# Ten sample tiles instead of nine in a DLRM interaction kernel, with layer 2 of the first two tiles placed between layers 0 and 1

## The reference, cut to what matters

```
e  = stack([tbl_m[ids[:, m]] for m in range(32)], axis=1)      # b m d
xk = e
for W in (W0, W1, W2):                                          # m h k, k = 64
    xk = relu(einsum('bmd,bhd,mhk->bkd', e, xk, W))
    outs.append(sum(xk, axis=2))
z = concatenate(outs, axis=1)                                   # 512 x 192
h = relu(concatenate([z, dense_ctx], 1) @ W_top1 + b_top1)      # 512
h = relu(h @ W_top2 + b_top2)                                   # 256
y = h @ W_top3
```

## Time and profile before

| | us |
|---|---|
| median of 3 runs | 350.59 (350.45 to 353.13) |
| the profiled execution | 353.74 |
| its span (first to last instruction) | 351.9 |
| TensorE busy | 305.4 (87%) |
| VectorE busy | 274.2 (78%) |
| GpSimd busy | 254.2 (72%) |
| ScalarE busy | 61.6 (18%) |

### The profile page before, as it was taken

How to read it: one execution, slowest core, us unless ns; L and a number is a source line. 1 busy time by engine, 2 the same in 40 slices (tenths; PEclk the granted TensorE clock), 3 DMA queues, 4 the chain that set the end, 5 groups by cost and what they waited for, 6 DMA issues and landing times. The chain is left out here.

```text
span 351.9 us, 3914 instructions
## 1 busy us (share of the span) xinstructions
PE 305.4 (87%) x1476; PEld 112.7 (32%) x1476; DVE 274.2 (78%) x173; ACT 61.6 (18%) x122; POOL 254.2 (72%) x193
## 2 busy tenths in 40 slices
PE   0016859798999988999999999999999999998986
PEld 0013513243334222323333333233333334333426
DVE  0024949799999969999999999999999788954201
ACT  1001210301220330012201220222031104113011
POOL 5775678879788988888898879898919567917000
PEclk9999996999999999999999999999999999999998
DMA  5374956957973984286338643952580102100000
GB/s 178 45 251 83 369 111 180 376 88 213 381 149 65 279 329 80 28 337 260 56 71 303 272 72 77 378 190 61 151 327 0 45 2 63 45 2 0 0 0 0
DMA packets 52282, 52.07 MB, mean 148 GB/s; under 512 B 37574, under 2 KB 42568, under 8 KB 49064
## 3 DMA queue, kind: packets, MB, share of 16 engines
q1 hardware_dynamic: 41272, 39.92, 34.2%
q10 hardware_dynamic: 6896, 10.85, 11.5%
q0 software_dynamic: 4096, 1.06, 3.0%
HBM read 41.33 MB, written 2.10 MB: 123 GB/s over the span
## 5 line engine op out<-in xcount | busy, mean ns | idle before, releaser
L519 DVE TENSOR_TENSOR z_vector<-left,r_forms 128x2048 f32<-128x2048 f32 (+3 forms) x140 | 260.0, 1924 | 45.4 <-DMA r_forms<-x_rows 23.0
L569 PE MATMUL result<-z_vector,w_sb 128*64 128x512 f32 (+2 forms) x1056 | 213.9, 557 | 41.5 <-DVE z_vector L519 40.2
L309 POOL DMA_INDIRECT gathered_rows<-table,row_index x128 | 121.8, 951 | 41.2 <-issue 34.5
L324 POOL TENSOR_TENSOR z_pool<-r_forms,xj_forms 128x1024 f32<-128x1024 f32 (+2 forms) x60 | 131.8, 2232 | 24.7 <-PE result L569 15.0
L569 PEld LDWEIGHTS result<-z_vector,w_sb 128*64 128x64 f32 x1056 | 77.3, 142 | 172.9 <-issue 143.4
L569 PE MATMUL result<-z_pool,w_sb 128*64 128x512 f32 (+2 forms) x240 | 51.8, 571 | 0.0
L384 ACT ACTIVATE x_sb<-result 128x512 f32<-128x512 f32 (+2 forms) x27 | 14.9, 551 | 169.7 <-PE result L569 169.7
L499 DVE TENSOR_REDUCE d_sums<-x_sb 128x32 f32<-128x512 f32 (+2 forms) x27 | 16.8, 625 | 20.0 <-ACT x_sb L384 20.0
L569 PEld LDWEIGHTS result<-z_pool,w_sb 128*64 128x64 f32 x240 | 15.7, 136 | 34.1 <-issue 33.2
L368 ACT ACTIVATE left<-xj_forms 128x512 f32<-128x512 f32 (+2 forms) x36 | 18.6, 547 | 17.1 <-DMA xj_forms<-x_sb 6.8
L359 ACT ACTIVATE left<-h_form 128x512 f32<-128x512 f32 (+2 forms) x18 | 10.0, 553 | 59.8 <-DVE z_vector L519 44.9
(11 more groups left out here) (32 smaller groups left out, 28.1 us busy)
## 6 DMA issues: line engine op xcount, KB each, us to landing
r_forms<-x_rows SPq DMA_DIRECT2D x24, 1024.0 KB, 10.4
r_forms<-x_rows SPq DMA_DIRECT2D x8, 768.0 KB, 6.8
xj_forms<-x_sb ACTq DMA_DIRECT2D x24, 256.0 KB, 4.0
h_form<-x_rows SPq DMA_DIRECT2D x12, 256.0 KB, 3.0
gathered_rows<-table,row_index POOLq DMA_INDIRECT x128, 3.3
r_forms<-x_rows SPq DMA_DIRECT2D x4, 512.0 KB, 6.1
x_rows<-gathered_rows SPq DMA_DIRECT2D x24, 64.0 KB, 2.5
xj_forms<-x_sb ACTq DMA_DIRECT2D x8, 192.0 KB, 3.1
```

The source lines that it names most:

```text
L309: nc.gpsimd.indirect_dma_start(gathered_rows[:, half % GATHERED, g], None, table, bass.IndirectOffsetOnAxis(ap=row_index[:, at:at + 1], ax ...
L324: nc.gpsimd.tensor_tensor(z_pool[:, unit % NZP, t, :, 0:columns(p)], r_form(q, p, t)[:, s0:s1], xj1_forms[form_buffer(n, p)][:, t, 0:colum ...
L519: nc.vector.tensor_tensor(z_vector[:, unit % NV, t, 0:s1 - s0, 0:columns(p)], left[:, t, bank, 0:columns(p)].unsqueeze(1).broadcast_to([12 ...
L569: done = nc.tensor.matmul(result[n][K * t:K * t + K, 0:columns(p)], weights, z[:, t, 0:columns(p)], start=first, stop=last)
```

## The change

The tiles become 8, 16, 24, six of 32, and 16: ten tiles. The order of the first four tiles is written out: (2, 0) comes ahead of (1, 1), and (2, 1) is cut in two, its r0 units ("form 0") between (0, 2) and (1, 2), its r1 units ("form 1") behind (0, 3). From p = 3 on the order is the old one. GpSimd has no products in (1, 0), (2, 0), (1, 1) and (2, 1), and makes the gathers of tiles 0 to 3 (40) ahead of its first product. The other tables of `pool_chunks` move up by one tile with the tiles. ScalarE's and TensorE's orders are written out in the same way.

```diff
-SAMPLES = [16, 24] + [32] * 6 + [24]
+SAMPLES = [8, 16, 24] + [32] * 6 + [16]
...
-STAGES = [(0, 0)]
-for _p in range(NP):
-    STAGES.append((1, _p))
+SPLIT = 1
+STAGES = [(0, 0, "all"), (1, 0, "all"), (0, 1, "all"), (2, 0, "all"), (1, 1, "all"), (0, 2, "all"), (2, 1, "form 0"),
+          (1, 2, "all"), (0, 3, "all"), (2, 1, "form 1")]
+for _p in range(SPLIT + 2, NP):
+    STAGES.append((1, _p, "all"))
     if _p + 1 < NP:
-        STAGES.append((0, _p + 1))
-    if _p > 0:
-        STAGES.append((2, _p - 1))
-STAGES.append((2, NP - 1))
-LAYERS = [_stage for _stage in STAGES if _stage[0] > 0]
-
-GATHERS_FIRST = GATHERS_BEFORE[6]
+        STAGES.append((0, _p + 1, "all"))
+    STAGES.append((2, _p - 1, "all"))
+STAGES.append((2, NP - 1, "all"))
+
+FORM0 = [(_n, _p) for _n, _p, _part in STAGES if _n > 0 and _part != "form 1"]
+FORM1 = [(_n, _p) for _n, _p, _part in STAGES if _part != "form 0"]
+
+GATHERS_FIRST = GATHERS_BEFORE[8]
...
-    few = {(1, 0): 0, (1, 1): 2, (2, 5): 4, (2, 6): 6, (2, 7): 6, (2, 8): 4}
+    few = {(1, 0): 0, (2, 0): 0, (1, 1): 0, (2, 1): 0, (1, 2): 2, (2, 6): 4, (2, 7): 6, (2, 8): 6, (2, 9): 4}
...
@@ GpSimd @@
-            pool.wait_ge(selected, 1)
-            for k in range(4):
-                gather(GATHERS_BEFORE[4] + 4 * k, GATHERS_BEFORE[4] + 4 * k + 4)
-                pool.wait_ge(z_vector_used, k + 2)
+            first = GATHERS_BEFORE[4]
+            pool.wait_ge(selected, selections(1, 0))
+            gather(first, first + 4)
+            pool.wait_ge(z_vector_used, VECTOR_AT[1, 0, 1] + 1)
+            gather(first + 4, first + 8)
+            pool.wait_ge(selected, selections(2, 0))
+            gather(first + 8, first + 12)
+            pool.wait_ge(z_vector_used, VECTOR_AT[0, 1, 0] + 1)
+            gather(first + 12, first + 16)
+            pool.wait_ge(selected, selections(1, 1))
+            gather(first + 16, first + 20)
+            pool.wait_ge(z_vector_used, VECTOR_AT[1, 1, 1] + 1)
+            gather(first + 20, first + 24)
+            pool.wait_ge(selected, selections(2, 1))
+            gather(first + 24, first + 28)
             first = GATHERS_FIRST
-            for n, p in STAGES:
+            for n, p in FORM1:
...
@@ VectorE @@
+            all_products(1, 0, [(0, 0)])
+            products(0, 1, 0)
+            all_products(2, 0, [(1, 0)])
+            all_products(1, 1, [(0, 1), (2, 0)])
+            products(0, 2, 0)
+            products(2, 1, 0)
+            products(2, 1, 1)
+            all_products(1, 2, [(0, 2), (1, 1)])
+            products(0, 3, 0)
+            for k in range(2, len(vector_units(2, 1))):
+                products(2, 1, k)
+            for p in range(SPLIT + 2, NP):
...
@@ TensorE @@
+            layer(1, 0)
+            select(2, 0)
+            vector_unit(0, 1, 0)
+            squares(1)
+            layer(2, 0, {1: [lambda: select(1, 1)]})
+            layer(1, 1)
+            select(2, 1)
+            vector_unit(0, 2, 0)
+            squares(2)
+            vector_unit(2, 1, 0)
+            vector_unit(2, 1, 1)
+            select(1, 2)
+            layer(1, 2)
```

More of the change, by code:

```diff
@@ L86, in pool_units @@
     return units + [(0, s, s + 2) for s in range(4 - max(0, chunks - 4), 4, 2)]
-VECTOR_BEFORE, POOL_BEFORE, STAGE_AT, LAYER_AT = {}, {}, {}, {}
-_v = _w = _l = 0
-for _k, _stage in enumerate(STAGES):
-    VECTOR_BEFORE[_stage], POOL_BEFORE[_stage], STAGE_AT[_stage] = _v, _w, _k
-    if _stage[0]:
-        LAYER_AT[_stage] = _l
-        _l += 1
-    _v += len(vector_units(*_stage))
+VECTOR_AT, POOL_BEFORE = {}, {}
+for _n, _p, _part in STAGES:
+    _count = len(vector_units(_n, _p))
+    for _k in {"all": range(_count), "form 0": range(2), "form 1": range(2, _count)}[_part]:
+        VECTOR_AT[_n, _p, _k] = len(VECTOR_AT)
+_w = 0
+for _stage in FORM1:
+    POOL_BEFORE[_stage] = _w
     _w += len(pool_units(*_stage))
@@ L445, in _ @@
             load_xj1(1, 0)
-            for p in range(NP - 1):
+            copy_xj1(1, 0)
+            copy_h(1)
+            relu(1, 0)
+            load_xj1(2, 0)
+            copy_xj1(2, 0)
+            relu(0, 1)
+            load_xj1(1, 1)
+            copy_xj1(1, 1)
+            relu(2, 0)
+            copy_h(2)
+            relu(1, 1)
+            load_xj1(2, 1)
+            relu(0, 2)
+            load_xj1(1, 2)
+            copy_xj1(1, 2)
+            copy_h(3)
+            relu(1, 2)
+            copy_xj1(2, 1)
+            relu(0, 3)
+            load_xj1(1, 3)
+            load_xj1(2, 2)
+            relu(2, 1)
+            for p in range(SPLIT + 2, NP - 1):
                 copy_xj1(1, p)
@@ L449, in _ @@
                 relu(1, p)
-                if p == 2:
+                if p == SPLIT + 2:
                     load_top()
-                if p > 0:
-                    copy_xj1(2, p - 1)
+                copy_xj1(2, p - 1)
                 relu(0, p + 1)
                 load_xj1(1, p + 1)
-                if p > 0:
-                    relu(2, p - 1)
+                relu(2, p - 1)
                 load_xj1(2, p)
@@ L527, in _, with all_products @@
                                            ALU.mult, ALU.add).then_inc(w0_folded, 1)
-            products(0, 0, 0)
-            for p in range(NP):
-                for k in range(len(vector_units(1, p))):
-                    products(1, p, k)
-                    if k == 1:
-                        sum_d(0, p)
-                        if p == 1:
-                            sum_d(1, 0)
-                        if p == NP - 1:
-                            sum_d(2, p - 2)
+            def all_products(n, p, sums=()):
+                for k in range(len(vector_units(n, p))):
+                    products(n, p, k)
+                    if k == 1:
+                        for of in sums:
+                            sum_d(*of)
+            products(0, 0, 0)
+            all_products(1, 0, [(0, 0)])
[10 more added lines that the diff above has]
+            for p in range(SPLIT + 2, NP):
+                sums = [(0, p)]
+                if p == SPLIT + 2:
+                    sums.append((1, p - 1))
+                if p == NP - 1:
+                    sums.append((2, p - 2))
+                all_products(1, p, sums)
                 if p + 1 < NP:
                     products(0, p + 1, 0)
-                    if p > 1:
-                        sum_d(2, p - 2)
-                if p > 0:
-                    for k in range(len(vector_units(2, p - 1))):
-                        products(2, p - 1, k)
-                        if k == 1:
-                            sum_d(1, p)
+                    sum_d(2, p - 2)
+                all_products(2, p - 1, [(1, p)])
             for k in range(len(vector_units(2, NP - 1))):
@@ L652, in _ @@
             pe.wait_ge(w12_loaded, 16)
-            for p in range(NP - 1):
-                layer(1, p, {1: [lambda: select(2, p - 1)]} if p > 0 else {})
+            layer(1, 0)
[11 more added lines that the diff above has]
+            layer(1, 2)
+            vector_unit(0, 3, 0)
+            squares(3)
+            for k in range(2, len(vector_units(2, 1))):
+                vector_unit(2, 1, k, k == len(vector_units(2, 1)) - 1)
+                if k == 2:
+                    select(1, 3)
+            for p in range(SPLIT + 2, NP - 1):
+                layer(1, p, {1: [lambda: select(2, p - 1)]})
                 vector_unit(0, p + 1, 0)
                 squares(p + 1)
-                if p > 0:
-                    layer(2, p - 1, {1: [lambda: select(1, p + 1)]})
-                else:
-                    select(1, 1)
+                layer(2, p - 1, {1: [lambda: select(1, p + 1)]})
             last = NP - 1
```

23 lines of the change are left out of this document (13 added, 10 removed).

## The result

The changed kernel takes **421.58 us** (median of 4 runs, 420.48 to 421.92), beside 351.01 us for the kernel before on the same chip: ratio 1.196 [1.190, 1.202]. The forecast was 428 us, in a range of 408 to 442. The profiled execution has a span of 420.1 us.

The account below looks back on a forecast made before the run. A loop from GpSimd's late gathers through five engines and queues was taken to bound it: tile 3 at 76.5, plus 46.3, plus four turns of 49.1, plus 2.8 + 114.7 - 7.8, span 428.9, less 1.3: 428 us (408 to 442).

Parts of the forecast that it names:

- E of tile 3: VectorE's end of layer 0 of tile 3, forecast at 76.5 us, bounds 73 and 81.
- to E of tile 4 (no clock loss): First turn of the gather loop, 46.3 us to 122.8; TensorE's idle time before (0, 3) is short, so full clock.
- four turns to E of tile 8: Tiles 5 to 8 each add 49.1 us, together 196.4, so (0, 8) ends at 319.2.
- Where the gathers stand: On GpSimd, tile p's second-half gathers move behind the products of (1, p-1), closing a loop once per tile.
- The length of a turn: Middle: 9.7 + 9.4 + 11.4 + 3.5 + 0.65 + 9.4 + 2.3 = 46.3 us per tile, before clock loss.
- The clock: TensorE's clock halves after each long stall, slowing (0, p): 2.8 us lost per turn, 49.1 us per period.
- The start: First select at about 22.4 us, (1, 2) starts on VectorE at 59.4, (0, 3) ends at 76.5.
- The end: After (0, 8): 2.8 us clock loss plus 114.7 as before, less 7.8 for the smaller last tile.
- A: Rival: the loop binds but TensorE's clock costs little; 414 us, chance 0.18.
- B: Rival: longer loop, all of (0, p) at half clock and landings of 10.8 us; 443 us, chance 0.10.
- C: Rival: gathers early enough, only start and end count, (1, 3) at 83 to 85; 345 to 350 us, chance 0.06.
- D: Rival: start waits shrink, forms keep up, tile 4's second half gathered by about 80 us; 341 us, chance 0.04.

Follow-up runs that it names:

- Late gathers alone: Kernel before, old tiles and layer order, with only GpSimd's gathers hung one product stage later: 422.87 us beside 363.25, ratio 1.164.
- filled run: Changed kernel with unread matmuls added on idle TensorE, 19, 13, 8, 11, 8 pairs for tiles 4 to 8: 415.76 us, ratio 1.173 beside 1.194 unfilled.
- last run with earlier gathers: Rerun of the changed kernel with 16 gathers instead of eight behind the products of (1, 2): 367.88 us beside 361.98, ratio 1.014.
- the sizes alone: Kernel before with only the new tile sizes, old order of stages: 355.55 us beside 352.33, ratio 1.009.
- the run with 17, 12, 8, 9, 8 pairs: Changed kernel with that many pairs of unread matmuls on TensorE ahead of (0, p), tiles 4 to 8: 431.66 us beside 430.54 unfilled.
- first run with earlier gathers: Changed kernel with eight more gathers ahead of GpSimd's first product: 374.7 us beside 363.95 for the kernel before, ratio 1.030.
- the first with 16 gathers behind (1, 2): Changed kernel with 16 gathers instead of eight behind the products of (1, 2), first of two runs: 372.33 us beside 363.25, ratio 1.029.

## Why the prediction was right

The forecast was 427.6, the median is 421.6. By its own steps, E being the end of layer 0 on VectorE:

| step | forecast | measured | off by |
|---|---|---|---|
| E of tile 3 | 76.5 | 79.8 | +3.3 |
| to E of tile 4 (no clock loss) | 46.3 | 45.0 | -1.3 |
| four turns to E of tile 8 | 196.4 | 188.6 | -7.8 |
| from there to the span's end | 109.7 | 106.7 | -3.0 |
| span | 428.9 | 420.1 | -8.8 |

The last line of the sum, the step from span to median, went the other way: I took 1.3 off the span, as before's median stood to its span; here the median is 1.5 above it. So of the 8.8 us by which the span was too long 2.8 were cancelled by luck, and inside the span the late start cancelled 3.3 of 12.1.

**Where the gathers stand: right.** GpSimd idles 12.4 to 14.4 us ahead of the products of (1, 3) to (1, 7), released by xj_forms, VectorE ahead of each (0, p), released by r_forms. Late gathers alone make the loop in the old kernel, earlier gathers take it away in the new one.

**The length of a turn: right in its links, 2 us too long.** In tile 6's turn: from E to the products 9.2 us without the clock's part against 9.7; products 9.37 as taken; gathers to the store 11.2 against 11.4; store to load 3.5 as taken; landing 8.2 against 9.4. The landing is the term that was mis-sized, 1.2 of the 2.1 us: I had read it from r0's loads in the steady middle (9.0, 9.4 and 10.8); in the five stalls it was 7.9 to 8.8. Why r0 lands sooner there no run says.

**The clock: right in kind, somewhat less.** Behind the five stalls the four pairs took 5.65, 6.17, 6.58, 6.58 and 5.21 us where 3.65 is full clock, so 1.6 to 2.9 lost, mean 2.4, where 2.8 was taken. The filled run gives 6.6 us for all five in the time; the intervals of the two ratios leave room for some 2.5 to 12. The Trainium skill ("TensorE: Matmul & The Clock Gate", Part 1) has the ramp under 1% of a typical kernel's span, which would be 4.2 us here. The slow passes add up to 11.9 us or 2.8%, more than that; what they cost in time, 6.6 us or 1.6%, is not clear of 1%, since 4.2 lies between 2.5 and 12.

**The start: 3.3 us too early.** (1, 2) was put at 59.4 on VectorE and began at 62.85, 3.4 us late. Half of it was there when (2, 1)'s first two units ended (57.8, put at 56.1), behind 1.95 us of waiting for tile 2's forms. The other half is the select, for which VectorE stood 5.02 us where 3.3 were allowed. I had given TensorE "about 2 more" at full clock, and its four pairs of (0, 2) were slow:

```profile
53.36 4.49 PE L621 MATMUL result<-z_vector,w_sb 128*64 128x384 f32 x16 [3.58 <-DVE z_vector L559]
```

Four pairs of that size took 2.80 us in the kernel before, at a granted clock of 1.00 (44 to 47 us); here it was 0.50 from 54 to 56 us. These 1.7 us are a fall of the clock in the start, which the sum had left out. (Its 22.4 for the first select should read 22.6, that is 31.61 less 9.0; the gather behind that select came at 22.55.)

**The end: 3.0 us too much.** 1.2 of it is the clock in (0, 8), 1.6 lost instead of 2.8. The other 1.8 lie behind layer 0 of tile 8: from the end of its squares to the end of the span the kernel before needed 110.2 us (from tile 7's squares) and the changed one 100.5, so the smaller last tile was worth 9.7 us where the sum took 7.8. Which stages gave the difference I have not broken down.

**The rivals.** A (the clock costs little, 414) was too low, since passes did slow down, though its number is nearly as close to 421.6 as the forecast. B's landing of 10.8 did not occur. C and D needed the gathers to be free of xj, and those of tiles 4 to 8 were not. C's (1, 3) at 83 to 85 came at 87.25. D's turning point, tile 4's second half gathered by about 80 us, was missed by far: they end at 108.

## What to carry to other kernels

When two producers share one in-order engine, write down for each thing it makes what the instruction ahead of it waits for; if that leads back to the thing's own earlier turn, add up the loop, in transfers and queues as well as in work. A loop of 47 us around engines with 35 us of work decides the time, and every engine in it, even one that is 59% busy, is then on the path. A count that paces one thing by another ("eight gathers behind each stage with products") must be counted anew when stages are moved or stop having products: here 8 gathers one stage earlier were worth 56 to 63 us.

## What the runs showed of the hardware

**Chips differ, most of it in the start.** The kernel before took 351.0 and 352.3 us on two chips and 362 to 364 on two others, one of them used twice (medians). The changed kernel's span on a slower chip was 8.5 us longer than on the first: 6.4 were there at the end of layer 0 of tile 4. On the slower chips the profile shows TensorE, in the first 100 us, standing for nothing it can name ("issue"), and never on the good ones; later labels of this kind there fall on the end of a VectorE product or are under 0.8 us. TensorE's group and first row in the changed kernel on the first chip, and in the last run with earlier gathers, on a slower one:

```profile
L621 PE MATMUL result<-z_vector,w_sb 128*64 128x512 f32 (+3 forms) x1208 | 230.9, 536 | 97.0 <-DVE z_vector L559 95.9
18.62 1.98 PE L621 MATMUL result<-z_vector,w_sb 128*64 128x128 f32 x16 [18.62 <-DVE z_vector L559]
```

```profile
L622 PE MATMUL result<-z_vector,w_sb 128*64 128x512 f32 (+3 forms) x1208 | 225.9, 521 | 44.7 <-issue 27.8
18.96 1.97 PE L622 MATMUL result<-z_vector,w_sb 128*64 128x128 f32 x16 [18.96 <-issue]
...
86.27 1.50 PE L622 MATMUL result<-z_vector,w_sb 128*64 128x512 f32 x5 [1.34 <-issue]
88.64 1.34 PE L622 MATMUL result<-z_vector,w_sb 128*64 128x512 f32 x2 [0.87 <-issue]
91.43 2.06 PE L622 MATMUL result<-z_vector,w_sb 128*64 128x512 f32 x3 [1.45 <-issue]
```

The 27.8 us must be read with care: 18.96 of them are the wait ahead of the very first matmul, which is as long on the good chip and has only another label there. What is left is about 9 us. TensorE goes on by two to five matmuls at a time with 0.9 to 1.5 us between, with its operands there: VectorE had made the last product it needed by 86.2, and the 16 records of (0, 3), which take 3.65 us elsewhere, end only at 96.8. That instructions reach TensorE too slowly is a guess; no run tests it. Dense transfers are not what goes with it at this place: the DMA share was 0.93 from 82 to 86 us, 0.49 from 86 to 90, and 0.09 from 90 to 94, where TensorE still stopped. What the change would be worth without the loop was therefore never measured as a whole on a good chip: it is 1.4 to 3% slower on the slower ones, and the sizes alone are 0.9% slower on a good one. That it would be faster than the kernel before is shown by nothing.

**The length of an idle time does not tell whether the clock falls.** In the run with 17, 12, 8, 9, 8 pairs, idle times of 2.36 to 3.87 us were followed by four pairs of 5.1 to 5.35 us, and 2.24 us by 3.65; in the last filled run 2.23 us was followed by 3.65. It looks like a border between 2.24 and 2.36 us, and it is none. The first run with earlier gathers, and the first with 16 gathers behind (1, 2):

```profile
146.61 3.65 PE L621 MATMUL result<-z_vector,w_sb 128*64 128x512 f32 x16 [2.96 <-DVE z_vector L559]
```

```profile
141.19 8.78 PE L622 MATMUL result<-z_vector,w_sb 128*64 128x512 f32 x32 [2.14 <-DVE z_vector L560]
```

Behind 2.96 us the four pairs kept full clock (granted 1.00 from 146 to 150 us). Behind 2.14 us the eight pairs, 7.04 at full clock, took 8.78 (granted 0.50 from 143 to 145 us). The idle time of 2.71 us ahead of (1, 3) is the same in ten traces; in seven of them, the changed kernel's first among them, the eight pairs took 8.5 to 8.8 us, in the three others TensorE ran them at full clock. The only idle time of this kind that I had used was 3.52 us. Idle times of 2 to 4 us may cost 1.5 us or nothing; only the granted clock of the pass behind them tells.
